# Expert gate and up projections as three float32r products of split operands, with the second weights fetched per tile

## The reference

```python
x = x + layernorm(attention(layernorm(x)))          # 16 heads of 16, RoPE, softmax, biases
x = x + layernorm(experts(layernorm(x)))

def experts(xs):                                    # E = 8, K = 2, D = 256, H = 684
    d2 = (xs * xs).sum(-1) + (centroid * centroid).sum(-1) - 2 * (xs @ centroid.T)
    w, sel = top_k(sqrt(max(d2, 1e-12)), 2)
    w = softmax(w)                                  # weight of each chosen expert
    out = 0
    for e in range(8):
        h = silu(xs @ Wg[e] + bg[e]) * (xs @ W1[e] + b1[e])
        out = out + we[:, e:e+1] * (h @ W2[e] + b2[e])
    return out
```

## Time and profile before

| | |
|---|---|
| Median of 3 runs (lowest, highest) | 1588.29 us (1581.68, 1606.2) |
| The profiled execution: time, span | 1573.55 us, 1571.8 us |
| Projections | 0 to 143 us |
| Attention, 16 groups | 143 to 791 us |
| O projection, layer norm | 791 to 868 us |
| Routing | 868 to 926 us |
| Loop over the 71 tiles | 926 to 1517 us |
| Tail | 1517 to 1571.8 us |

### The profile page before, as it was taken

The page is one execution under the profiler, slowest core; times in us unless marked ns, Lnnn a source line. Parts: engine busy times, 40 slices in busy tenths (PEclk is TensorE's granted clock), DMA queues, the critical chain, the costliest instruction groups (busy, mean ns, idle before and its releaser), DMA issues.

```text
span 1571.8 us, 29999 instructions
## 1 busy us (share of the span) xinstructions
PE 1435.0 (91%) x9435; PEld 792.5 (50%) x9436; DVE 1110.0 (71%) x1983; ACT 846.7 (54%) x1613; POOL 431.5 (27%) x417
## 2 busy tenths in 40 slices
PE   7899999999999999999999259999999999999950
PEld 5454333333333333333355136777777777777740
DVE  6989999999999999997037764555545555555425
ACT  4523888888888888887856322222222222222215
POOL 5750000000000010001024143444444444444425
PEclk9999999999999999999999659999999999999985
DMA  6986364334636454640458804222221222222236
GB/s 205 263 222 116 77 170 97 60 73 75 100 57 123 65 90 65 102 70 26 148 90 205 281 25 96 33 30 33 33 33 31 33 33 31 33 33 33 32 88 197
DMA packets 125116, 141.80 MB, mean 90 GB/s; under 512 B 55131, under 2 KB 98949, under 8 KB 125030
## 3 DMA queue, kind: packets, MB, share of 16 engines
q1 hardware_dynamic: 109126, 121.98, 33.7%
q0 software_dynamic: 15904, 18.66, 7.5%
HBM read 86.30 MB, written 54.30 MB: 89 GB/s over the span
## 4 chain that ended last, share of the span: by engine, by line
PE 79%; DVE 7%; issue 5%; ACT 4%; POOL 2%; DMA 1%; SPq 1%; DVEq 0%; POOLq 0%; ACTq 0%
PE psum L1687 21%; PE psum L1525 17%; PE psum L1551 16%; PE psum L1706 12%; PE psum L1697 3%; PE psum L1618 2%; DVE mx L955 2%; PE psum L1537 2%; ACT work L1344 1%; PE psum L1616 1%; PE psum L1499 1%; ACT weights L1354 1%; PE psum L1485 1%; PE psum L1673 1%; PE psum L1637 1%
## 5 line engine op out<-in xcount | busy, mean ns | idle before, releaser
L955 DVE TENSOR_REDUCE mx<-psum 128x1 f32<-128x1024 f32 x512 | 621.8, 1222 | 19.1 <-PE psum L1525 16.7
L1344 ACT ACTIVATE work<-psum 128x512 f32<-128x512 f32 x1024 | 556.4, 597 | 80.6 <-PE psum L1537 18.1
L1525 PE MATMUL psum<-stack 48*128 48x512 f32 x1024 | 372.9, 445 | 6.6 <-DVE mx L955 6.1
L1537 PE MATMUL psum<-stack 50*128 50x512 f32 x1024 | 375.4, 446 | 0.0
L1687 PE MATMUL psum<-weights,values 128*128 x1136 | 341.1, 453 | 0.6 <-DVE values L1174 0.6
L1551 PE MATMUL psum<-work,values 128*32 128x256 f32 x4096 | 328.6, 393 | 9.2 <-ACT weights L1354 9.2
L1687 PEld LDWEIGHTS psum<-weights,values 128*128 128x128 f32 x1136 | 211.3, 191 | 99.6 <-issue 3.1
L1525 PEld LDWEIGHTS psum<-stack 48*128 48x128 f32 x1024 | 151.3, 185 | 217.1 <-DVE mx L955 183.6
L1421 ACT ACTIVATE values<-values 128x342 f32<-128x342 f32 x142 | 69.3, 488 | 250.5 <-DVE values L1186 250.5
L1706 PE MATMUL psum<-weights,work 114*128 (+1 forms) x852 | 198.6, 383 | 1.2 <-ACT work L1432 0.8
L1551 PEld LDWEIGHTS psum<-work,values 128*32 128x32 f32 x4096 | 82.2, 108 | 197.2 <-ACT work L1344 101.2
(11 more groups left out here) (184 smaller groups left out, 1185.4 us busy)
## 6 DMA issues: line engine op xcount, KB each, us to landing
stack<-qk_scr SPq DMA_DIRECT2D x192, 128.0 KB, 6.2
qk_scr<-weights SPq DMA_DIRECT2D x16, 1024.0 KB, 4.8
weights<-in_w SPq DMA_DIRECT2D x8, 1368.0 KB, 6.6
ot_scr<-weights SPq DMA_DIRECT2D x16, 512.0 KB, 3.2
weights<-in_w SPq DMA_DIRECT2D x8, 684.0 KB
work<-in_b SPq DMA_DIRECT2D x8, 684.0 KB, 8.8
y_d<-zeros SPq DMA_DIRECT2D x1, 4224.0 KB, 14.0
v_scr<-weights SPq DMA_DIRECT2D x32, 128.0 KB, 2.4
```

The costliest lines, as they stand in the source:

```text
L955: dve.tensor_reduce(mx[:, r, a, t:t + 1], bank(4 + 2 * a, 2), AX, ALU.max, negate=True).then_inc(s_max, 1)
L1344: act.activation(pt[u % 4][:, j, :], bank((c + HG * u + n) % 3), ACT.Exp, scale=SC).then_inc(s_exp, 1)
L1525: ins = pe.matmul(bank(4 + 2 * a + half), qs[t3][at:at + QROWS, r, P * t:P * (t + 1)], ks[t3][at:at + QROWS, r, 512 * half:512 * (half + 1 ...
L1537: pe.matmul(bank((t3 + HG * u + n) % 3), ks[t3][at:at + MROWS, r, P * st:P * (st + 1)], qs[t3][at:at + MROWS, r, 512 * half:512 * (half + ...
```

## The change

Five things change together.

- The weights of gate and up are split into a high part (the value rounded to float32r) and a low part (the rest), both float32r. `gate_up` computes high·high, high·low and low·high, in three blocks of 456 columns: 18 products in place of 8 in float32. DVE splits the turned x rows into their two parts.
- The biases are folded into the last weight row. POOL sets the last element of every normed row that goes to DRAM to 1.0 (`set_ones`; `keep` waits for it); row 255 of the weights is subtracted from the other rows and the bias takes its place, which gives the same sum because a row of xs adds up to nothing. DVE's four bias additions per tile go, silu and the multiplication read PSUM.
- The split costs a pass over the weights, which is made during attention. In groups 0 to 7, behind the max rows, SP loads one expert's raw weights (`load_raw`: 128 rows, 127 rows, the bias row, and row 255 to all partitions). POOL splits them in the next group, between `split_max` of pair 0 and of pair 1 (`split_weights`). Six of the eight are parked in DRAM (`park`, 2.8 MB each, groups 2 to 7) since the SBUF space is in use until attention ends, and loaded again: one in group 13, the others behind the O projection, the last at the loop's start.
- The second weights no longer fit. In groups 8 to 11 they are repacked in DRAM as 115 rows (114 and the bias) of 1536 numbers for each expert, and in the loop SP fetches the tile's expert anew for each tile (`stream_w2`, 115 rows, 707 KB) into one of two buffers, as soon as `down(t-2)` is done.
- All of x2 is stored ahead of the routing, and read back during the loop in two pieces (`x2_back`, issued at tiles 32 and 64), so the tail reads only the sums.

The diff, cut to its core:

```diff
@@ -40,6 +40,11 @@
 SC = D ** -0.5
 CH = HID // 2
 KH, KP = 6, HID // 6
+CG = 2 * HID // 3
+TAIL = HID - CG
+WSIZE = 2 * KC * 2 * HID
+JOBS = (3, 4, 5, 6, 7, 2, 0, 1)
+PARKED = 6
 NS = 2 * NTOK // P + E - 1
...
         other_stacks = [placed(f"stack{n + 1}", stack_shape, F32R, total + stack_at * n) for n in range(2)]
         stack = [first_stack] + other_stacks
-        weights = sb("weights", [P, total])
...
+        def load_raw(sp, n):
+
+            e = JOBS[n]
+            after(sp, s_wl, KC * n)
+            sp.dma_start(raw[:, 0, :], w1[e, 0:P, :]).then_inc(s_raw, 16)
+            sp.dma_start(raw[0:P - 1, 1, :], w1[e, P:C - 1, :]).then_inc(s_raw, 16)
+            sp.dma_start(raw[P - 1:P, 1, :], b1[e].rearrange("(a n) -> a n", a=1)).then_inc(s_raw, 16)
+            sp.dma_start(raw[:, 2, :], w1[e, C - 1, :].partition_broadcast(P)).then_inc(s_raw, 16)
+
+        def park(sp, n):
+
+            sp.wait_ge(s_wh, KC * (n + 1))
+            sp.wait_ge(s_wl, KC * (n + 1))
+            after(sp, s_park, 16 * n)
+            sp.dma_start(w1_d[n], w1_sb[:, n % 2].rearrange("p h k n -> p (h k n)").bitcast(F32)).then_inc(s_park, 16)
+
+        def load_w1(sp, n, done=s_w):
+            sp.wait_ge(s_park, 16 * PARKED)
+            sp.dma_start(w1_sb[:, JOBS[n]].rearrange("p h k n -> p (h k n)").bitcast(F32), w1_d[n]).then_inc(done, 16)
+
+        def stream_w2(sp, t, q):
+
+            e = sp.value_load(tile_e[0:1, bass.ds(t, 1)], min_val=0, max_val=E - 1)
+            if not isinstance(t, int) or t > 1:
+                sp.wait_ge(s_yp, t - 1)
+            sp.dma_start(w2_sb[q].rearrange("p k n -> p (k n)"),
+                         w2_d[bass.ds(e, 1), :, :].rearrange("a p n -> (a p) n")).then_inc(s_w2[q], 16)
 
...
-                if g == 0:
-                    load_w1(sp, 3)
-                elif g == 1:
+                if g < E:
+                    load_raw(sp, g)
+                if g == 13:
+                    load_w1(sp, 5)
+
+                if 0 <= g - 2 < PARKED:
+                    park(sp, g - 2)
+                if g == 1:
                     sp.dma_start(y_d.rearrange("(n p) d -> p n d", p=P),
                                  zeros[:, :].rearrange("p (a d) -> p a d", a=1).to_broadcast([P, NT + 1, C])).then_inc(s_yc, 16)
                 elif g == 5:
                     load_wo(sp)
-                if g in (2, 8, 14):
-                    load_w1(sp, (g - 2) // 6)
-
-                elif g in (4, 6, 12):
-                    load_w2(sp, {4: 4, 6: 6, 12: 5}[g])
+                if 8 <= g < 12:
+                    for e in range(2 * (g - 8), 2 * (g - 7)):
+                        sp.dma_start(w2_d[e, 0:KP, :].rearrange("p (k n) -> p k n", k=KH),
+                                     w2[e].rearrange("(k p) n -> p k n", p=KP)).then_inc(s_w2p, 16)
+                elif g == 12:
+                    sp.dma_start(w2_d[:, KP, 0:C], b2).then_inc(s_w2p, 16)
+                    sp.dma_start(w2_d[:, KP, C:].rearrange("e (a n) -> e a n", n=C),
+                                 zeros[0:E, :].rearrange("p (a n) -> p a n", a=1).to_broadcast([E, KH - 1, C])).then_inc(s_w2p, 16)
 
             groups(sp, during)
             sp.wait_ge(s_sp, BLOCKS * (NG - 1))
...
-                    load_w2(sp, u - 11)
-                if u == 13:
-                    load_w1(sp, E - 4)
+                keep(u)
+                if u == 8:
+                    sp.wait_ge(s_vg, NG)
+                    load_w1(sp, 2)
             sp.wait_ge(s_x2, NT // 2)
-            sp.dma_start(x2_d.rearrange("(n p) d -> p n d", p=P)[:, kept:, :], x2[:, kept:, :]).then_inc(s_x2s, 16)
+            sp.dma_start(x2_d.rearrange("(n p) d -> p n d", p=P), x2).then_inc(s_x2s, 16)
             sp.wait_ge(s_op, NT // 2)
-            for e in range(E - 3, E - 1):
-                load_w1(sp, e)
+            for n in range(2):
+                load_w1(sp, n)
             sp.wait_ge(s_x2s, 16)
-            for e in range(early):
-                load_b1(sp, e)
+            sp.wait_ge(s_dd, 1)
+            load_w1(sp, 3)
             sp.wait_ge(s_wc, 1)
             sp.dma_start(w_d[0:2 * NTOK, :].rearrange("(a p) o -> a (p o)", p=P), w_turned).then_inc(s_wd, 16)
+            sp.wait_ge(s_w2p, 16 * (E + 2))
...
-            load_w2(sp, E - 1, s_last)
-            load_w1(sp, E - 1, s_last)
+            load_w1(sp, 4, s_last)
+
+            def stream(lo, hi):
+
+                with sp.Fori(lo, hi) as i:
+                    for q in range(2):
+                        stream_w2(sp, 2 * i + q, q)
+
+            x2_rows = x2_d.rearrange("(n p) d -> p n d", p=P)
+            stream(1, NT // 2 + 1)
+            sp.wait_ge(s_gu, 3 * NT)
+            sp.dma_start(x2_back[:, 0:20, :], x2_rows[:, 0:20, :]).then_inc(s_x2b, 16)
+            stream(NT // 2 + 1, NT + 1)
+            sp.wait_ge(s_gu, 3 * 2 * NT)
+            sp.dma_start(x2_back[:, 20:NT, :], x2_rows[:, 20:NT, :]).then_inc(s_x2b, 16)
+            stream(NT + 1, NS // 2)
+            if NS % 2:
+                stream_w2(sp, NS - 1, 0)
 
 
...
@@ -781,11 +834,27 @@
                     dims, inverses = [ot[b % 2][:, part, :, 512 * half:512 * (half + 1)] for part in range(2)]
                     pool.tensor_tensor(dims, dims, inverses, ALU.mult).then_inc(s_div, 1)
 
+            def split_weights(n):
+
+                high, low = w1_sb[:, n % 2, 1], w1_sb[:, n % 2, 0]
+                pool.wait_ge(s_raw, 64 * (n + 1))
+                after(pool, s_park, 16 * (n - 1))
+                pool.tensor_tensor(raw[:, 0, :], raw[:, 0, :], raw[:, 2, :], ALU.subtract).then_inc(s_sub, 1)
+                pool.tensor_tensor(raw[0:P - 1, 1, :], raw[0:P - 1, 1, :], raw[0:P - 1, 2, :], ALU.subtract).then_inc(s_sub, 1)
+                for k in range(KC):
+                    pool.wait_ge(s_sub, KC * n + k + 1)
+                    pool.tensor_copy(high[:, k, :], raw[:, k, :]).then_inc(s_wh, 1)
+                for k in range(KC):
+                    pool.wait_ge(s_wh, KC * n + k + 1)
+                    pool.tensor_tensor(low[:, k, :], raw[:, k, :], high[:, k, :].bitcast(F32), ALU.subtract).then_inc(s_wl, 1)
+
             def during(i, c):
                 g = over(i, c, 1)
                 if not (isinstance(g, int) and g + 1 >= NG):
-                    for r in range(PAIRS):
-                        split_max(g + 1, r)
+                    split_max(g + 1, 0)
+                    if 0 < g <= E:
+                        split_weights(g - 1)
+                    split_max(g + 1, 1)
                 if not (isinstance(g, int) and g + 2 >= NG):
                     copy_values(i, c + 2)
                 if g in (9, 13):
...
+            def set_ones(u):
+
+                pool.wait_ge(s_t3, u + 1)
+                pool.memset(xn2[u % 4][:, :, C - 1:C], 1.0).then_inc(s_one, 1)
+
...
@@ -1170,39 +1248,27 @@
 
             def save_xt2(t):
                 dve.wait_ge(s_mt, t + 1)
-                after(dve, s_gu, 4 * t)
-                dve.tensor_copy(x_t.rearrange("p k t -> p (k t)"), bank(6)[:, 0:C]).then_inc(s_mx, 1)
+                after(dve, s_gu, 3 * t)
+                rows = bank(6)[:, 0:C]
+                dve.tensor_copy(x_high.rearrange("p k t -> p (k t)"), rows).then_inc(s_xh, 1)
+                dve.wait_ge(s_xh, t + 1)
+                dve.tensor_tensor(x_low.rearrange("p k t -> p (k t)"), rows, x_high.rearrange("p k t -> p (k t)").bitcast(F32),
+                                  ALU.subtract).then_inc(s_mx, 1)
                 dve.wait_ge(s_wg, 16 * (t + 1))
                 dve.tensor_copy(w_all[:, bass.ds(t, 1)], w_slot[:, :]).then_inc(s_wk, 1)
 
+            def hidden(t):
+
+                dve.wait_ge(s_si, 2 * t + 2)
                 after(dve, s_ht, t)
-                dve.tensor_tensor(hid[:, CH * c:CH * (c + 1)], bank(2 * c + 1)[:, 0:CH], bias(HID), ALU.add).then_inc(s_ub, 1)
-
-            def multiply(t, c):
...
             def gate(t):
-                for c in range(2):
-                    act.wait_ge(s_gb, 2 * t + c + 1)
-                    act.activation(gates[c], gates[c], ACT.Silu).then_inc(s_si, 1)
+                after(act, s_hid, 2 * t)
+                act.wait_ge(s_gu, 3 * t + 1)
+                act.activation(gates[:, 0:CG], bank(0)[:, 0:CG], ACT.Silu).then_inc(s_si, 1)
+                act.wait_ge(s_gu, 3 * t + 2)
+                act.activation(gates[:, CG:HID], bank(1)[:, 0:TAIL], ACT.Silu).then_inc(s_si, 1)
...
@@ -1679,60 +1744,65 @@
             def gate_up(t, e):
 
                 pe.wait_ge(s_mx, t + 1)
-                for c in range(4):
-                    col = (c % 2) * HID + (c // 2) * CH
-                    after(pe, (s_gb, s_ub)[c % 2], 2 * (t - 1) + c // 2 + 1)
-                    dst = bank(c)[:, 0:CH]
+                for c in range(3):
+                    if c < 2:
+                        after(pe, s_si, 2 * (t - 1) + c + 1)
+                    if c > 0:
+                        after(pe, s_hid, 2 * (t - 1) + c)
+                    dst = bank(c)[:, 0:CG]
```

(14 more changed lines are left out.)

167 lines of the change are left out of this document (77 added, 90 removed).

## The result

| | before | changed |
|---|---|---|
| Median (lowest to highest) | 1584.99 (1580.42 to 1606.2), 4 runs | 1849.46 (1842.71 to 1868.66), 4 runs |
| Ratio, 95% interval | | 1.170 [1.161, 1.180] |
| Profiled execution, span | 1573.55, 1571.8 | 1868.66, 1866.9 |

The account below looks back on a forecast made before the run. PE, busy 91% of the span, was taken as the bound. 1571.8 + 112 (attention) + 43 (loop) + 5 (held-up gathers) - 6 (tail) = 1726, 1728 with 1.75 around it; put at 1735 us, range 1595 to 1860.

Parts of the forecast that it names:

- both causes: In attention 127 raw rows on one engine delay PE, +112 us; in the loop the weights' fetch delays gathers, +43 us.
- My own forecast: Whole kernel: raw rows slow attention and the fetch holds up gathers; 1735 us, own range 1685 to 1800, chance 0.48.
- the second rival: In the loop every gather is held up by the fetch: 10.4 us a tile, +165 us, 1850 in all; chance 0.08.
- One engine for 127 rows: In attention, 127 being prime, that raw load's 695 KB lies on one engine, which needs 31.5 us for its 788 KB.
- The ring: Attention: raw load, POOL's split, max rows, next raw load take 55 us against a group's 40.1; eight cost +112 us.
- my upper bound: Attention's worst case, +185 us: parked weights and the stacks' loads also queue on the raw rows' engine in each group.
- The 7 us of slack: Attention: the first long group uses up about 7 us of slack, taken off the 119 us that eight would cost.
- Gates: Loop: gate and up as 18 products take 3.46 us a tile, not 4.60; -81 us if PE stays the bound.
- The loop: The fetch on five engines holds up the gather in every second tile: 8.67 us a tile, +43 us, not -81.
- The first rival: Loop: the gather isn't held up, engines taking turns between queues; PE stays the bound, 1604 to 1625 us; chance 0.32.
- O projection and routing: Stretch between attention and loop: `set_ones` and `keep` covered by idle POOL, 0; repacking and reloading 0, at most +10 us.
- The clock: Loop: PE's clock may fall behind a late gather, as to 0.66 over 10 us before; counted only in the upper bound.

## Why the prediction was right, and where it was not

- **The number.** The direction and both causes were right, and the range held, with 11 us to spare. My own forecast of 1685 to 1800 did not hold. That the second rival (every gather held up) had 1850 is chance: it needs 10.4 us a tile, and the tile took 8.98; the missing time lay in attention and between attention and the loop.
- **One engine for 127 rows: right, and shown.** The share was 0.06 behind the raw loads, and spreading them took 195 us away.
- **The ring's length: mis-sized,** the step that carried most of the error. 55 us was the value, 64.2 is what it measured, so 193 us in place of 119. The leg from the raw load to POOL was 45.6 and not 32.8: the split waits for the parking store too, whose share is on that engine. POOL and the max rows were put 4 us too high together (17.3 + 3.9 + 1 against 14.7 + 3.5; a cast took 1.33 us), which hid a third of that. The parking store and the other loads on this engine were in my upper bound (+185), and I took neither.
- **A second way round the ring was not in it at all.** In the first ring, which has no parking store, the leg to POOL (243.19 to 277.22) was 34.0 us, about as forecast, and the ring was still 60.7 us long (to 303.88). SP stood for 23.07 us at the store of the outputs (259.75), so the max rows of pair 0 were stored only at 289.25, and those of pair 1, which stand behind them in SP's stream, at 301.14. That the spread cured this too is what the 40.1 us of all eight groups show.
- **The 7 us of slack** can't be seen: the first group with a split was 61.3 us long, 21 more than before, and the mean of all eight 24 more.
- **Gates: 18 in 3.72 us** against 3.46, 0.207 each; a tile's PE work is 7.19 and not 6.93. Weight loads weren't exposed as the upper bound of 5.4 had it.
- **The loop: the cause right, the path only in part, the size by luck.** That the gathers are late because of the fetch is shown by three runs: spread 7.98, none 7.29, other order 7.31. The first rival (not held up) falls by the same. But the mean of 8.98 is near to 8.67 since three misses cancel in part: gates 0.26 us a tile more, waits for the gather 1.12 where 1.74 was forecast (3.47 in every second tile), and 0.67, most of it clock, that was in no sum. And the gather of rows in such a tile was mostly 5.5 to 7.4 us on its way, not 7.7 (10.4 less 2.7); the rest is that it was issued late, because the row weights' gather was held up as well. The forecast had only one of the two gathers. The Trainium skill (DMA: Bandwidth & Descriptors, "Queues, rings and completion order") has an engine take turns between its queues packet by packet; these traces neither show such turns nor rule them out. If they helped the gather, it was not enough.
- **O projection and routing: +35 where 0 was forecast.** With both loads spread this stretch took 147 us; the changed kernel took 24 us more, and its windows at half clock with PE busy (1005 to 1034, 1070 to 1092) are worth about that. Of the 11 left, 3 are the first gather behind the first two fetches (5.87 us in place of 2.88), and about 8 lie ahead of routing, where PE waits for ACT and ACT, by the code, for the stores of normed rows (the profile names no releaser). `set_ones` was costed at nothing with POOL's idle time as cover. POOL did have the time; what I missed is that a wait stands behind it, for SP's stores and the loads queued behind them. Without the ones PE's gaps there are gone; how much of the 8 us they are is not shown.
- **The clock: not in the sum at all,** only a mention in the upper bound. It is some 38 us of the loop, about 24 of the stretch before it, 6 in group 14 (50.5 us against 44.6 in the kernel before) and most of the +9 ahead of the first store: it was 0.50 from 145 to 165 there, and in the kernel with both loads spread too, whose first store came at 197.1. Together that is about a quarter of the 295 us.
- The tail, -5 for -6, was right.

## What to carry to other kernels

Look at the row count of every transfer before its bytes: 127 rows on one engine made a group 64 us long where 112 and 15 left it at 40, and two such splits moved the kernel from 17% slower to even. When a periodic transfer is added to a loop of small gathers, place it in time: issued behind the gather it was free, ahead of it it cost 0.7 us a tile, and on five engines neither place was free. Follow every gather of the loop, the small one of the row weights too: what waits for it may be the one that issues the next. And a wait of PE can cost more than its length: behind one of 2.46 us `down` took 1.8 us longer, at 0.50 of the clock. When a leg of a ring is a queue, sum everything that the queue serves in that time, not only the transfer that the ring is waiting for, and look for a second way round it.

## What the runs showed that I had not expected

- The granted clock stayed at 0.50 for 15 to 40 us in which PE was busy throughout. In the kernel with the raw rows spread, behind a gap of about 1.5 us:

```profile
566.00:600.00 34.00, 34.00 (x192) 10.72 (x190) 20.18 (x18) 17.96 (x33) 0.42 (x2) 0.50 0.33 59
```

  The kernel before has a like gap at the same place and stayed at 1.00:

```profile
562.00:600.00 38.00, 37.19 (x364) 13.71 (x360) 37.15 (x34) 33.38 (x63) 2.13 (x5) 1.00 0.49 79
```

  Such a stretch costs 10 to 18 us (half its length), and comes in some executions and not in others: it began the O projection in three of the profiles here, and not in the others. What decides it is open; the runs within one kernel spread by 10 to 50 us, which is of that size.
- SP stood for 13 us at the issue of the one bias row, and for up to 23 at other issues, while one engine had its 127 rows to do. So one full engine seems to hold up the issuing queue, and with it transfers for the fifteen others; with the rows spread SP took 0.4 us for each of these issues.
